# First attention: the last unit's mask added from PSUM by VectorE, and the first unit's splits one step later

## The reference, cut to what matters

```python
scores = jnp.einsum('bhqd,bhkd->bhqk', Q, K) / jnp.sqrt(jnp.float32(D_K))
scores = jnp.where(mask, -jnp.inf, scores)          # mask: (1, 1, 512, 1024)
attn_w = jax.nn.softmax(scores, axis=-1)
attn_w = jnp.where(jnp.isnan(attn_w), 0.0, attn_w)
out = jnp.einsum('bhqk,bhkd->bhqd', attn_w, V)
```

## Time and profile before

| | |
|---|---|
| three runs | 1187.74 us median, 1185.92 to 1192.19 |
| the profiled execution | 1191.78 us, span 1190.1 us |
| mean granted TensorE clock | 0.973 |
| TensorE busy | 1120.6 us, 94% |
| VectorE busy | 548.0 us, 46% |
| ScalarE busy | 455.2 us, 38% |
| GpSimd busy | 417.7 us, 35% |
| first attention, first to last step | from 81 us to 301 us |
| its last unit, by weighted sums | from 281.12 us to 299.52 us |

### The profile page before, as it was taken

The page is one execution under the profiler, slowest core; times in us unless marked ns, Lnnn a source line. Parts: engine busy times, 40 slices in busy tenths (PEclk is TensorE's granted clock), DMA queues, the critical chain, the costliest instruction groups (busy, mean ns, idle before and its releaser), DMA issues. The chain is left out here.

```text
span 1190.1 us, 19179 instructions
## 1 busy us (share of the span) xinstructions
PE 1120.6 (94%) x7157; PEld 720.2 (61%) x7178; DVE 548.0 (46%) x1534; ACT 455.2 (38%) x626; POOL 417.7 (35%) x454
## 2 busy tenths in 40 slices
PE   7899999998899999999899999999986899999996
PEld 4553333332578888888674333333325899999996
DVE  4568787875641111111357767666407112121211
ACT  4457667776441111111143565555654011111110
POOL 4347888784047782000013000000201233333331
PEclk9889999998999999999989999999998899999999
DMA  8634222002266954353177222100004999989970
GB/s 218 155 96 82 41 40 41 1 1 79 98 213 164 356 203 153 141 194 71 48 235 161 41 41 38 34 12 1 1 1 164 307 376 349 333 304 310 311 231 2
DMA packets 88551, 168.02 MB, mean 141 GB/s; under 512 B 11026, under 2 KB 61412, under 8 KB 86036
## 3 DMA queue, kind: packets, MB, share of 16 engines
q1 hardware_dynamic: 79860, 155.24, 41.7%
q0 software_dynamic: 6048, 8.28, 2.9%
q10 hardware_dynamic: 2560, 3.41, 1.0%
HBM read 148.09 MB, written 19.54 MB: 141 GB/s over the span
## 5 line engine op out<-in xcount | busy, mean ns | idle before, releaser
L1453 ACT ACTIVATE prob<-st_ps 128x1024 f32<-128x1024 f32 x256 | 254.0, 1022 | 169.0 <-PE st_ps L1321 105.0
L246 DVE CUSTOM_DVE_ANT_0 junk<-s_ps,bias_rows,mx 128x512 f32<-128x512 f32 x240 | 170.5, 748 | 53.9 <-PE s_ps L231 53.1
L231 PE MATMUL s_ps<-k_stack,q_stack 97*128 97x512 bf16 x476 | 177.7, 386 | 7.0 <-ACT q_stack L275 5.4
L246 DVE CUSTOM_DVE_ANT_0 junk<-s_ps,bias_rows 128x512 f32<-128x512 f32 x236 | 154.9, 688 | 60.1 <-PE s_ps L231 59.4
L1311 PE MATMUL st_ps<-q_stack,k_stack 100*128 100x512 bf16 x512 | 171.9, 385 | 4.7 <-ACT prob L1453 2.5
L1868 PE MATMUL h_ps<-expert_in,w 128*128 (+1 forms) x704 | 153.4, 379 | 1.7 <-DMA w<-in_w 1.0
L1337 PE MATMUL o_ps<-prob,v_unit 128*32 128x512 f32 x1024 | 140.7, 606 | 8.4 <-DVE prob L1484 4.4
L1868 PEld LDWEIGHTS h_ps<-expert_in,w 128*128 128x128 f32 (+1 forms) x704 | 131.4, 187 | 22.3 <-issue 2.4
L1271 POOL TENSOR_TENSOR prob<-prob,keep_cols 128x1024 int32<-128x1024 int32 x56 | 132.3, 2364 | 30.8 <-ACT prob L1453 30.8
L231 PEld LDWEIGHTS s_ps<-k_stack,q_stack 97*128 97x128 bf16 x476 | 45.3, 98 | 140.4 <-DVE mx L246 84.0
L2303 ACT ACTIVATE silu<-gu_ps 128x512 f32<-128x512 f32 x46 | 27.5, 597 | 227.3 <-PE gu_ps L2240 227.3
(11 more groups left out here) (353 smaller groups left out, 1294.5 us busy)
## 6 DMA issues: line engine op xcount, KB each, us to landing
wg<-in_gateT SPq DMA_DIRECT2D x23, 1024.0 KB, 6.3
wu<-in_upT SPq DMA_DIRECT2D x23, 1024.0 KB, 9.1
wd<-in_downT SPq DMA_DIRECT2D x23, 1024.0 KB, 12.7
w<-in_w SPq DMA_DIRECT2D x16, 1368.0 KB
w<-in_w SPq DMA_DIRECT2D x8, 1280.0 KB
k_stack<-k_scr SPq DMA_DIRECT2D x16, 384.0 KB, 5.0
k_stack<-k_scr SPq DMA_DIRECT2D x16, 256.0 KB, 5.7
k_scr<-k_parts SPq DMA_DIRECT2D x24, 128.0 KB, 2.7
```

Of the source, the lines that this page charges most:

```text
L231: pe.matmul(self.ps[:, self.bank("job", u, j)], stack(self.pr.Q[b], MROW, i % 2, h, slice(qt * P, (qt + 1) * P)), stack(self.pr.K[b], MROW ...
L246: self.pr.nc.vector.tensor_tensor_reduce(out=self.junk[:, self.bank("job", u, j)], in0=self.ps[:, self.bank("job", u, j)], in1=self.m.bias ...
L1453: nc.scalar.activation(prob[:, kt % 2, 2 * hp:2 * hp + 2], st_ps[:, 2 * hp:2 * hp + 2], ACT.Exp).then_inc(exp_done, 1)
```

## The change

In the last unit of the first attention (steps 0 to 6), heads 0 and 1 are no longer masked behind the exponential. VectorE adds `m.bias_hi` to their scores while they lie in PSUM and writes the sums to `prob`; ScalarE then takes the exponential in place there, after that of heads 2 and 3. Head 2 is no longer `unbiased`: it gets a bias matmul as head 3 does. The semaphore `kept_last` gives way to `masked`, which also tells TensorE that the banks of heads 0 and 1 may be written again. In the first unit, the first split moves from behind `keep` of step 1 to behind that of step 2, the second from step 4 to step 5, and `values` from step 2 to step 0.

```diff
-        kept, kept_last = pr.sem(f"kept{l}"), pr.sem(f"kept_last{l}")
+        kept, masked = pr.sem(f"kept{l}"), pr.sem(f"masked{l}")
...
             if l == 1 or (u == NU - 1 and kt == KT - 1):
                 return False
-            return h < (3 if u == NU - 1 else 2)
+            return h < 2
...
                             keep(u, kt)
-                            if kt == (2 if u == 0 else 0):
+                            if kt == 0:
                                 values(u + 1, *divmod(u + 1, B))
-                            if kt == 1:
+                            if kt == (1 if u else 2):
                                 row.cut(pool, u + 1, (u + 1) % B, 0)
-                            if kt == 4:
+                            if kt == (4 if u else 5):
                                 row.cut(pool, u + 1, (u + 1) % B, 1)
...
                     i, b = divmod(u, B)
-                    if h % 2 == 0:
+                    if l == 0 and u == NU - 1 and kt and h == 0:
+                        pe.wait_ge(masked, kt)
+                    elif l == 0 and u == NU - 1 and kt and h == 2:
+                        pe.wait_ge(exp_done, u * 16 + kt * 2 + 1)
+                    elif h % 2 == 0:
                         pe.wait_ge(exp_done, u * 16 + kt * 2 + h // 2 + 1)
...
                         pe.wait_ge(kept, u * KT + kt + 1)
-                    elif l == 0 and kt < KT - 1:
-                        pe.wait_ge(kept_last, 2 * kt + 2)
...
+                def exps(n, hp):
+                    act.wait_ge(st_ready, 2 * n + hp + 1)
+                    nc.scalar.activation(prob[:, n % 2, 2 * hp:2 * hp + 2], st_ps[:, 2 * hp:2 * hp + 2],
+                                         ACT.Exp).then_inc(exp_done, 1)
+
+                def exps_masked(n, kt):
+                    act.wait_ge(masked, kt + 1)
+                    nc.scalar.activation(prob[:, n % 2, 0:2], prob[:, n % 2, 0:2], ACT.Exp).then_inc(exp_done, 1)
+
                 for u in range(NU):
                     for kt in range(KT):
-                        for hp in range(2):
-                            if hp == 0:
-                                act.wait_ge(pv_done, u * 8 + kt + 1)
-                            act.wait_ge(st_ready, u * 16 + kt * 2 + hp + 1)
-                            nc.scalar.activation(prob[:, kt % 2, 2 * hp:2 * hp + 2], st_ps[:, 2 * hp:2 * hp + 2],
-                                                 ACT.Exp).then_inc(exp_done, 1)
+                        n = u * KT + kt
+                        act.wait_ge(pv_done, n + 1)
+                        if l == 0 and u == NU - 1 and kt < KT - 1:
+                            exps(n, 1)
+                            exps_masked(n, kt)
+                        else:
+                            exps(n, 0)
+                            exps(n, 1)
...
                     for kt in range(KT - 1):
-                        keep = keep_cols[:, kt]
-                        dve.wait_ge(exp_done, (NU - 1) * 16 + kt * 2 + 3)
-                        pair = prob[:, kt % 2, 0:2]
-                        nc.vector.scalar_tensor_tensor(out=pair, in0=pair, scalar=BIG,
-                                                       in1=keep.unsqueeze(1).broadcast_to([P, 2, SQ]),
-                                                       op0=ALU.min, op1=ALU.mult).then_inc(kept_last, 1)
-                        dve.wait_ge(exp_done, (NU - 1) * 16 + kt * 2 + 4)
-                        third = prob[:, kt % 2, 2]
-                        nc.vector.scalar_tensor_tensor(out=third, in0=third, scalar=BIG, in1=keep,
-                                                       op0=ALU.min, op1=ALU.mult).then_inc(kept_last, 1)
+                        n = (NU - 1) * KT + kt
+                        dve.wait_ge(st_ready, 2 * n + 1)
+                        dve.wait_ge(pv_done, n + 1)
+                        nc.vector.tensor_tensor(prob[:, kt % 2, 0:2], st_ps[:, 0:2],
+                                                m.bias_hi[:, kt].unsqueeze(1).broadcast_to([P, 2, SQ]),
+                                                ALU.add).then_inc(masked, 1)
```

## The result

The changed kernel takes 1183.68 us (median of 20 runs, 1179.32 to 1191.08), the kernel before 1190.25 us (20 runs beside them, 1185.05 to 1195.66). The ratio is 0.995, with a 95% interval from 0.9933 to 0.9967: 4 to 8 us faster. The border of 0.5% that the prediction drew between a change and none lies inside that interval. The profiled execution took 1186.85 us, its span is 1185.2.

The account below looks back on a forecast made before the run. TensorE, busy for 94% of the span, was taken as the bound. Savings of 5.88 us in the last unit and 1.3 in the first made 7.2, taking the median from 1187.74 to 1180.5 us, range 1177 to 1185.5.

Parts of the forecast that it names:

- The border of 0.5%: Whole kernel: a change of 5.9 us, at 1181.8 us, about what a measurement can tell from none.
- the stated range: Whole kernel: 1177 to 1185.5 us, leaving out the lower part of the blocked-addition case and the slower-than-before case.
- the forecast's own: Whole kernel: range of 1177.5 to 1183 us for the forecast without its rivals, given a chance of 0.62.
- the first rival: Last unit: GpSimd blocks VectorE's new addition as it did the masks; 1182.7 or 1184.9 us, middle 1184, chance 0.08.
- The addition isn't blocked: Last unit: VectorE's addition from PSUM loses nothing to GpSimd's addition and takes 1.25 us.
- the other reading, by the operand's place: Last unit: the SBUF mask, as second tensor, takes the port shared with GpSimd, which makes the sum 1184 us.
- The beat of 2.40 us: Last unit: TensorE sets the pace at 3.50 minus 5 x 0.22 us a step; six steps make 14.40 us.
- The first unit: First unit: moving the splits and the values copy saves 0.35 and 0.95 us, together 1.3 us.
- my upper bound of 1.61: First unit: the most the new order could save, both TensorE idles, 0.50 + 1.11 us.
- the last unit's: Last unit: six steps at 2.40 us take 14.40 against 20.28 us, 5.88 us less.
- the 0.50 stretch: Last unit: second step, TensorE busy throughout at the 1.2 GHz level after idling; its loss counted within the 5.88 us.
- The rival with the clock behind the attention: After the attention: a later start shifts where TensorE falls to 1.2 GHz, 4.8 us per stretch, ending slower; chance 0.03.

Follow-up runs that it names:

- the run with the collision put back: Changed kernel plus one VectorE addition of 512 columns from two SBUF inputs, directly ahead of step 1's mask addition; ratio to the kernel before 0.9984.

## Why the prediction was right, and where it was off

The forecast was 1180.5 us from a median of 1187.74, 7.2 us less. Measured are 6.6 us between the medians and 6.0 by the ratio. The result, 1183.68 us, lies 3.2 us above the forecast, inside the stated range and just outside the forecast's own (to 1183). Of the 3.2 us 2.5 are the kernel before, which came out at 1190.25 over 20 runs instead of 1187.74 over three; 0.7 are the change's. By itself the time would fit the first rival (middle 1184) better than the forecast. It's the profile that decides between them.

The range wasn't added up soundly. 2 us for the median and the bounds named beside it (0.3 earlier; 1.4 and 1.3 later) give 1178.2 to 1185.2 if they are simply added, not 1177.5 to 1183. So 1183 was too narrow an end for the forecast's own range by the prediction's own bounds.

- The addition isn't blocked: shown, 1.22 and 1.23 us in the midst of GpSimd's. The rows that carried this were L246 and L2006, and the run with the collision put back shows that an instruction of the other kind at that place is blocked. The Trainium skill ("SBUF — State Buffer", section "SBUF: two separate sides") puts the lock on VectorE instructions with two SBUF inputs, against GpSimd instructions that read SBUF. The traces agree: 5.00 us with two SBUF inputs, 1.23 with one input from PSUM, and a memset of 1.39 us that the pair mask didn't hold up. The mask in SBUF as second operand did not block it, so the other reading, by the operand's place, falls here.
- The beat of 2.40 us, worked out by taking five matmuls from a step of 3.50, was met to 0.01, and six steps took 14.42 against 14.40. The exponential from SBUF took 1.05 us beside 1.02 for the one from PSUM, and the two together, 276.94 to 278.91, 1.97 where I had 1.98. The addition took 1.22 or 1.23 us where I had 1.25. The 0.06 us that I gave to the input from PSUM isn't its price: L246 has a second form in the kernel before, also from PSUM but without the starting maximum `mx` as an input, and that one takes 688 ns, as 512 columns from SBUF do.

```profile
L246 DVE CUSTOM_DVE_ANT_0 junk<-s_ps,bias_rows 128x512 f32<-128x512 f32 x236 | 154.9, 688 | 60.1 <-PE s_ps L231 59.4
```

- The first unit gained 1.58 us against 1.3. The waits for the split are 0.17 and 0.16 us where I gave 0.15 each; the transposes themselves start 0.24 us later in their step (3.73 us after the sum before them, where it was 3.49). What I had missed is in my favour: a weighted sum that waits for nothing runs into the transposes ahead of it. From the first transpose (93.20) to the matmul behind the sum (94.60) are 1.40 us, where I had 0.61 for the transposes and 1.00 for the sum, one behind the other. That is 0.21 us at each of the two places. The idle 1.61, less twice 0.24, and twice 0.21 back make 1.55 of the 1.58. That the total came close to my upper bound of 1.61 is a coincidence of these terms.
- Off was the size of one term: the last unit's. In the profile that I worked from it was 5.88 us by forecast and 5.86 measured, but that profile had the longest low clock. Three profiles hold the old last unit, at 24.41, 23.18 and 23.36 us. The difference to 18.55 is 5.9, 4.6 and 4.8, 5.1 on the mean. With the first unit's 1.6 that makes 6.7 us where I said 7.2, next to the medians' 6.6; the interval of 4 to 8 us holds both. The step that was off is taking the cost of the 0.50 stretch, which follows the stall, from one execution.
- The rival with the clock behind the attention came to nothing that the change brings: the stretch behind it varies over 4 us by itself.
- What was not seen: how much of the gain is the order's own. Taking GpSimd's long addition away gives 18.70 us with the old masks. The new instructions are worth 0.15 us by themselves; they are a way around the port, and one bias matmul alone went about two thirds of it (4.06 of 5.86 us).

## What to carry to other kernels

When a VectorE instruction takes seven times its usual length and waits for no semaphore, look at what GpSimd, which shares the port with VectorE, runs at that moment. In the last unit, in every run, two SBUF inputs on VectorE and an SBUF read on GpSimd excluded each other, and the later one paid. The cure was an operand that comes from PSUM; another moment for the long GpSimd instruction should do as well, since without it the loss was gone. Cost the beat of a TensorE-bound loop from a neighbouring step with a known number of matmuls. And take what a stall costs through the clock from more than one profile: the idle time repeats, the low clock after it doesn't.

## What the runs showed of the hardware

- A VectorE instruction of 512 columns with two SBUF inputs that met a running GpSimd addition ended 0.55 us after it, whatever its start (3.27 and 5.00 us instead of 0.69). One that met GpSimd's copy ended 0.38 us after it (1.43 us). Begun 0.03 us ahead of GpSimd's addition, it kept its length and the addition took 5.06 instead of 4.56 us.
- A VectorE addition with one input in PSUM ran at its usual length in the midst of GpSimd's addition (1024 columns, bfloat16 mask, 1.23 us). So did a product with a float32 input in SBUF inside other GpSimd instructions that read SBUF (256 columns, 0.42 us).
- GpSimd's memset of 1536 columns (1.39 us) and VectorE's pair mask from SBUF (1.23 us) overlapped at full speed.
- TensorE's granted clock stayed at 1.00 after 1.73 us of idling, and fell to 0.50 after 3.97 us, and for some of the time (means 0.82 and 0.80 in two steps) after 2.63 us. After the same stall, 3.97 or 3.98 us of idling, the second step ran at a mean of 0.50 in one execution, of 0.59 in another and of 0.56 in a third (with the first unit's new order).
